# A decoder layer on one core: the cross-attention context as one product of 448 columns, its results in two bank halves, added on GpSimd

## The reference

```
q = rmsnorm((x @ Wq).reshape(b, s, H, D), gq)
k = rmsnorm((ctx @ Wk).reshape(b, Skv, H, D), gk)
v = (ctx @ Wv).reshape(b, Skv, H, D)
attn = softmax(einsum('bqhd,bkhd->bhqk', q, k) / sqrt(D))
out = einsum('bhqk,bkhd->bqhd', attn, v).reshape(b, s, H * D) @ Wo
```

## Time and profile before

| what | us |
|---|---|
| runs of the kernel | 1050.33 (median), 1049.07, 1054.15 |
| the profiled execution | 1048.38 |
| its span, first to last instruction | 1046.6 |
| PE, PEld busy | 1018.7, 909.6 |
| DVE, ACT, POOL busy | 725.7, 537.0, 531.0 |

### The profile page before, as it was taken

How to read it: one execution, slowest core, us unless ns; L and a number is a source line. 1 busy time by engine, 2 the same in 40 slices (tenths; PEclk the granted TensorE clock), 3 DMA queues, 4 the chain that set the end, 5 groups by cost and what they waited for, 6 DMA issues and landing times.

```text
span 1046.6 us, 20309 instructions
## 1 busy us (share of the span) xinstructions
PE 1018.7 (97%) x7021; PEld 909.6 (87%) x7021; DVE 725.7 (69%) x1496; ACT 537.0 (51%) x1075; POOL 531.0 (51%) x515
## 2 busy tenths in 40 slices
PE   8999989999999999999999999999999999999997
PEld 8866568899999999999999999999987888888885
DVE  4378866777767767776776776766886576666648
ACT  5355546655455455555554554555553346676610
POOL 1257857754644643634634634634474545544544
PEclk9999999999999999999999999999999999999999
DMA  8100104324323223233233233234220779999843
GB/s 299 62 32 2 61 18 157 150 109 155 115 107 114 100 107 117 96 111 115 94 116 109 99 118 104 103 116 132 103 90 1 278 284 380 388 400 388 303 116 115
DMA packets 45274, 153.46 MB, mean 147 GB/s; under 512 B 3769, under 2 KB 4793, under 8 KB 42145
## 3 DMA queue, kind: packets, MB, share of 16 engines
q1 hardware_dynamic: 42976, 145.38, 38.5%
q0 software_dynamic: 2240, 7.34, 2.1%
HBM read 130.04 MB, written 22.66 MB: 146 GB/s over the span
## 4 chain that ended last, share of the span: by engine, by line
PE 73%; POOL 4%; DVE 4%; issue 2%; ACT 1%; POOLq 0%; DVEq 0%; ACTq 0%
PE xa_y_ps L86 6%; PE xa_y_ps L88 5%; PE xa_y_ps L87 5%; PE ex_raw_gu_ps L86 5%; PE ex_raw_gu_ps L88 4%; PE ex_raw_gu_ps L87 4%; PE xa_c_ps L1965 4%; PE xa_c_ps L1961 4%; PE xa_c_ps L1960 3%; PE ex_raw_ey_ps L2187 3%; PE xa_turn_ps L2042 3%; PE xa_turn_ps L1998 3%; PE front_k_ps L86 3%; PE front_k_ps L88 3%; PE front_k_ps L87 3%
## 5 line engine op out<-in xcount | busy, mean ns | idle before, releaser
L1275 POOL TENSOR_TENSOR xa_probs<-xa_probs,xa_inv_sum 112x750 f32<-112x750 f32 x63 | 97.7, 1552 | 75.7 <-DVE xa_inv_sum L1615 75.7
L1564 DVE TENSOR_TENSOR xa_kT_lo<-xa_turn_ps,xa_kT_hi 128x750 fp32r<-128x750 f32 x63 | 59.2, 940 | 99.8 <-ACT xa_kT_hi L1363 99.7
L1260 POOL TENSOR_TENSOR k_ms<-k_ss,sum_eps 125x6 f32<-125x6 f32 x63 | 12.5, 198 | 210.9 <-DVE k_ss L1580 210.9
L1960 PE MATMUL xa_c_ps<-xa_probsT_hi,xa_nat 125*128 125x224 f32 x384 | 92.3, 274 | 2.7 <-ACT xa_probsT_hi L1379 2.7
L1961 PE MATMUL xa_c_ps<-xa_probsT_hi,xa_nat 125*128 125x224 f32 x384 | 92.3, 275 | 0.0
L1379 ACT CAST xa_probsT_hi<-xa_turn_ps 125x672 fp32r<-125x672 f32 x62 | 44.6, 720 | 87.3 <-PE xa_turn_ps L2042 87.3
L1263 POOL TENSOR_TENSOR k_inv<-k_ms,neg_half 125x6 f32<-125x6 f32 x63 | 83.4, 1324 | 8.3 <-POOL k_ms L1260 6.6
L1385 ACT ACTIVATE xa_probs<-xa_scores_ps,xa_bias,xa_q_scale 112x375 f32<-112x375 f32 x126 | 82.8, 663 | 5.9 <-DVE xa_bias L1590 4.7
L1960 PEld LDWEIGHTS xa_c_ps<-xa_probsT_hi,xa_nat 125*128 125x128 f32 x384 | 73.6, 192 | 3.5 <-issue 3.1
L1961 PEld LDWEIGHTS xa_c_ps<-xa_probsT_hi,xa_nat 125*128 125x128 f32 x384 | 73.5, 191 | 0.5
L86 PE MATMUL front_k_ps<-land_xa_wk_hi,land_xa_ctx 128*125 128x256 f32 x252 | 71.4, 283 | 1.5 <-DVE front_k_hat L1607 1.2
(11 more groups left out here) (406 smaller groups left out, 3545.8 us busy)
## 6 DMA issues: line engine op xcount, KB each, us to landing
xa_nat<-ctx_split SPq DMA_DIRECT2D x56, 750.0 KB
ex_raw_raw<-in_w_units SPq DMA_DIRECT2D x15, 1408.0 KB, 8.1
ex_raw_raw<-in_w_units SPq DMA_DIRECT2D x15, 768.0 KB, 8.0
land_ex_raw<-in_w_units SPq DMA_DIRECT2D x8, 1408.0 KB, 8.2
land_ex_raw<-in_w_units SPq DMA_DIRECT2D x8, 768.0 KB, 7.9
ctx_split<-xa_nat SPq DMA_DIRECT2D x8, 750.0 KB
sorted_x<-ex_raw_y_sb SPq DMA_DIRECT2D x7, 768.0 KB, 10.3
ex_raw_x_nat<-sorted_x SPq DMA_DIRECT2D x21, 256.0 KB, 8.4
```

The source lines that it names most:

```text
L1275: pool.tensor_tensor(probs[0:T, u % 2], probs[0:T, u % 2], inv_sum[0:T, u % 2, :].unsqueeze(2).broadcast_to([T, 2, KV]), ALU.mult).then_in ...
L1564: dve.tensor_tensor(kT_lo[:, :, 0:KV], turn_ps[:, :, 0:KV], kT_hi[:, :, 0:KV].bitcast(F32), ALU.subtract).then_inc(sem["kT_lo_done"], 1)
L1960: pe.matmul(c_view[:, c], nat[0:KT, u % 2, 0, at], probsT_hi[0:KT, :, cols], start=(t == 0), stop=False)
```

## The change

In units 8 to 61 the context product is done by `context_pairs`. The high and the low transposed probabilities of a unit now lie next to each other in one buffer, `probsT`. For each half `c`, the high context is multiplied with both in one matmul of 448 columns per third of the keys; the low context is multiplied with the high probabilities as before, in 224 columns. The result of a half `c` so has two parts of 224 columns: high x high plus low x high, and high x low. They fill a bank of their own: half 0 goes to `c_ps`, half 1 goes to the second bank of `turn_ps`.

In even units half 0 starts with the matmuls that need no low probabilities: three with the low context, one of the high context and the high probabilities; then come the wait for `probsT_lo_done`, one matmul of 224 columns and two of 448. Half 1, and both halves of odd units, are three of 448 and three of 224 columns, and begin behind the wait for `probsT_lo_done`.

ScalarE copies the first part of each half to `cT_hi` and the second part to a new buffer `c_second`. VectorE subtracts `cT_hi` from the first part of each half, into `c_rest`. GpSimd adds `c_rest` and `c_second` into `cT_lo`, first thing in its slot. TensorE waits at the turn of k for `c_rest_done` and `c_second_done` of the unit, since both read the second bank of `turn_ps` (`second_bank_read`). Units 0 to 7, 62 and 63 keep `context_of`.

```diff
-        probsT_hi, probsT_lo = sb("probsT_hi", [P, 2, KT_N * T], F32R), sb("probsT_lo", [P, 2, KT_N * T], F32R)
+        probsT = sb("probsT", [P, 2, 2, KT_N * T], F32R)
+        probsT_hi, probsT_lo = probsT[:, 0], probsT[:, 1]
+        c_second = sb("c_second", [P, CC, 2, T])
+        c_rest = y_sb[:, 1, 0:CC * 2 * T].rearrange("p (c h t) -> p c h t", c=CC, h=2)
...
+        c_pair = [bank[:, 0:4 * T].rearrange("p (l h t) -> p l h t", l=2, h=2) for bank in (c_ps, turn_ps[:, 1])]
...
             def slot(s, i):
+                u = s - 3
+                if B <= u < N:
+                    part = slice(u % 2 * T, (u % 2 + 1) * T)
+                    hold(pool, sem["c_rest_done"], i, CC * B, CC * (u - B + 1))
+                    hold(pool, sem["c_second_done"], i, CC * B, CC * (u - B + 1))
+                    pool.tensor_tensor(cT_lo[:, :, :, part], c_rest, c_second[:], ALU.add).then_inc(sem["cT_lo_done"], 1)
                 if s % B == 4 and s // B + 1 < PAIRS:
...
+                    for c in range(CC if u >= B else 0):
+                        hold(act, sem["c_ready" if c else "c0_ready"], i, B, u + 1)
+                        act.copy(cT_hi[:, c, :, u % 2 * T:(u % 2 + 1) * T], c_pair[c][:, 0]).then_inc(sem["cT_hi_done"], 1)
+                        hold(act, sem["cT_lo_done"], i, B, u)
+                        act.copy(c_second[:, c], c_pair[c][:, 1]).then_inc(sem["c_second_done"], 1)
...
-                    hold(dve, sem["cT_hi_done"], i, B, u + 1)
                     part = slice(u % 2 * T, (u % 2 + 1) * T)
-                    dve.tensor_tensor(cT_lo[:, :, :, part], c_view, cT_hi[:, :, :, part].bitcast(F32),
-                                      ALU.subtract).then_inc(sem["cT_lo_done"], 1)
+                    if u < B:
+                        context_low(u)
+                    for c in range(CC if u >= B else 0):
+                        hold(dve, sem["c_second_done"], i, CC * B, CC * (u - B) + c + 1)
+                        hold(dve, sem["cT_lo_done"], i, B, u)
+                        dve.tensor_tensor(c_rest[:, c], c_pair[c][:, 0], cT_hi[:, c, :, part].bitcast(F32),
+                                          ALU.subtract).then_inc(sem["c_rest_done"], 1)
...
+            context_halves(u - 2)
...
+            def context_sum(u):
+
+                part = slice(u % 2 * T, (u % 2 + 1) * T)
+                dve.wait_ge(sem["c_rest_done"], CC * (u - B + 1))
+                dve.wait_ge(sem["c_second_done"], CC * (u - B + 1))
+                dve.tensor_tensor(cT_lo[:, :, :, part], c_rest, c_second[:], ALU.add).then_inc(sem["cT_lo_done"], 1)
...
+            context_rest(u - 2)
...
+            context_sum(u - 2)
...
+            def context_pairs(u, i):
+
+                context_loaded(u, i)
+                if u == B:
+                    pe.wait_ge(sem["cT_lo_done"], B)
+                hold(pe, sem["c_rest_done"], i, CC * B, CC * (u - B) - 1)
+                hold(pe, sem["c_second_done"], i, CC * B, CC * (u - B) - 1)
+                hold(pe, sem["probsT_hi_done"], i, B, u + 1)
+                cols = [slice(t * T, (t + 1) * T) for t in range(KT_N)]
+                if u % 2 == 0:
+                    for t in range(KT_N):
+                        pe.matmul(c_pair[0][:, 0], nat_part(u, 1, 0, t), probsT_hi[0:KT, :, cols[t]], start=(t == 0), stop=False)
+                    pe.matmul(c_pair[0][:, 0], nat_part(u, 0, 0, 0), probsT_hi[0:KT, :, cols[0]], start=False, stop=False)
+                    hold(pe, sem["probsT_lo_done"], i, B, u + 1)
+                    pe.matmul(c_pair[0][:, 1], nat_part(u, 0, 0, 0), probsT_lo[0:KT, :, cols[0]], start=False, stop=False)
+                    for t in range(1, KT_N):
+                        mm = pe.matmul(c_pair[0], nat_part(u, 0, 0, t), probsT[0:KT, :, :, cols[t]], start=False, stop=(t == KT_N - 1))
+                    mm.then_inc(sem["c0_ready"], 1)
+                hold(pe, sem["probsT_lo_done"], i, B, u + 1)
+                for c in range(u % 2 == 0, CC):
+                    if c == 1:
+                        squares_taken(i, u + 2, 1)
+                    for t in range(KT_N):
+                        pe.matmul(c_pair[c], nat_part(u, 0, c, t), probsT[0:KT, :, :, cols[t]], start=(t == 0), stop=False)
+                    for t in range(KT_N):
+                        mm = pe.matmul(c_pair[c][:, 0], nat_part(u, 1, c, t), probsT_hi[0:KT, :, cols[t]], start=False,
+                                       stop=(t == KT_N - 1))
+                    mm.then_inc(sem["c_ready" if c else "c0_ready"], 1)
+
+            def second_bank_read(u, i):
+
+                hold(pe, sem["c_rest_done"], i, CC * B, CC * (u - B + 1))
+                hold(pe, sem["c_second_done"], i, CC * B, CC * (u - B + 1))
...
+                    if s - 3 >= B:
+                        second_bank_read(s - 3, i)
...
-                    context_of(u, i)
+                    if u < B:
+                        context_of(u, i)
+                    else:
+                        context_pairs(u, i)
...
+            second_bank_read(N - 3, 0)
```

47 lines of the change are left out of this document (32 added, 15 removed).

## The result

The changed kernel takes 1077.21 us (median of 1074.15, 1077.72, 1076.70 and 1078.47); the kernel before, with one more execution beside the three of the table, took 1051.68 us. The ratio is 1.0246 (95% interval 1.0220 to 1.0273): slower. The profiled execution took 1074.15 us against 1048.38, 25.8 us more, with a mean granted clock of 0.999 in both. The other three executions of the changed kernel were 2.6 to 4.3 us longer than the profiled one, and their mean granted clock was 0.997 or 0.998. So TensorE ran longer at its lower level in them; where, no trace shows.

The account below looks back on a forecast made before the run. TensorE's stream was taken as the bound (PE busy 97% of the span). Terms -6.4 + 4.6 + 4.7 + 21.3 (both stops) + 0.5 = 24.7 us, added to a median of 1050.33, gave 1075 us; range 1061 to 1090.

Parts of the forecast that it names:

- Merged matmuls: Context products, units 8 to 61: 297 mergers of two 224-column matmuls into one of 448 save 0.0214 us each, 6.4 us.
- The earlier wait for the low probabilities: Even units' context: the wait moves from behind six matmuls to behind four, costing 0.17 us each, 4.6 us in all.
- odd units ... pay nothing: Odd units' context: 12 query matmuls stand ahead of it, so the earlier wait costs nothing there.
- The second bank in an ordinary slot: Turn of k in ordinary slots: TensorE waits 0.1 us for the bank holding half 1, 4.7 us in all.
- a way to PE: From an end on DVE to PE's next weight load: at most 0.23 us, taken as 0.05.
- First stop: Split slots with wq: the sum delays POOL's queue, so TensorE waits 1.8 us for k_hat, in six slots.
- Second stop: Turn behind the split slot: TensorE waits 1.93 us for c_rest, queued behind wo_lo; net 1.5 us, seven times.
- the low end of the term: Turn behind the split slot: wo_lo at 1.42 us instead of 2.16 shortens the stop by 0.7 us, 5 us in all.
- Straight code: Code behind the loop: it takes its pieces twice more, for 0.5 us.
- the clock: Rival, split slots: two near stops lower TensorE's clock, 3 us more per split slot, 21 in all, 1096; chance 0.04.
- The other three: Rivals: bank waits in every slot (1089, chance 0.12); only the second stop (1064, 0.08); stops absent, faster side (1044, 0.10).

Follow-up runs that it names:

- e7: Changed kernel with each 448-column context product written as two of 224, same banks and waits: 1080.21 us, ratio 1.0283 to the kernel before.
- e10: e5 with the first context half of even units not merged, its six high-probability products ahead of the wait: 1046.06 us, ratio 0.9974 to the kernel before.
- e8: Kernel before plus only an unused 448-column GpSimd sum, behind a wait for the context's low part, heading six split slots: 1060.12 us, ratio 1.0105.
- e1: Changed kernel with GpSimd's split of wo's high part moved behind k_inv in every split slot: 1075.18 us, ratio 1.0234 to the kernel before.
- e3: Changed kernel with VectorE's split of wo's low part moved behind the context's subtractions in the next slot: 1071.52 us, ratio 1.0199 to the kernel before.
- e11: Changed kernel with only the last units (58 to 61) back in the form of before: 1067.65 us, ratio 1.0169 to the kernel before.
- e4: Changed kernel with both moves, wo's high part behind k_inv and its low part behind the context's subtractions: 1061.34 us, ratio 1.0109 to the kernel before.
- e9: Changed kernel with two unused VectorE reductions ahead of the first context subtraction in slot 37 and every eighth: 1082.29 us, ratio 1.0318 to the kernel before.
- e2: Changed kernel with VectorE's bias written as two instructions of one tensor input each: 1081.16 us, ratio 1.0282 to the kernel before.
- e5: Changed kernel with wo_hi on ScalarE, wo_lo behind c_rest, units 58 to 61 in the old form: 1047.93 us, ratio 0.9985 to the kernel before.

## Why the prediction came out as it did

The time was forecast at 1075 and measured at 1077.2, the profiled execution at 1073.1 and 1074.15. The mechanism is right; part of the closeness is luck, since errors cancel. By stage: up to slot 60 the terms gave some 22.5 us and 17.3 were measured (from one split slot to the next 3.7, and it was 3.0); for slots 61 to 64 they gave 2.2 and it was 5.8; for the experts nothing, and it was 3.1. The other half of the 2.2 us between forecast and median comes from the step from profile to median: 1.95 us was carried over from the kernel before, and in the changed kernel it is 3.06, in executions with a lower granted clock.

- **Merged matmuls, -6.4.** Right in kind and rate. The spacing is 0.203 us, and e7 gives 0.10 to 0.12 us a slot. The Trainium skill (TensorE: Matmul & The Clock Gate, "Back-to-back issue gap") has 2.5 ns a merger in a formula that it gives for an isolated matmul, and says that the formula under-counts short ones in a stream with weight loads; taken as the prediction took it, it would be 0.015 us a slot, and the runs show eight times that.
- **The earlier wait for the low probabilities, 0.17 us in even units.** Right: 0.17 in the rows, 0.19 by e7, and e10 got it back. The step that failed is "odd units ... pay nothing". It was read in slots with query products and carried to the last pair, which has none: there the wait grew by 1.24 and 0.99 us.
- **The second bank in an ordinary slot, 4.7.** Wrong in size: nothing. By e7 an odd slot pays 0.00. The fit put the end of `c_rest` 1.29 us into the slot, called it a draw against the turn's weight load at 1.33, and added a way to PE. In the changed kernel it ends 1.22 us into the slot (508.53 + 0.39 in slot 36) and the load stands at 1.35. This is most of the 5.2 us by which the term up to slot 60 was too dear.
- **First stop, 1.8.** Size 1.72 - 0.08 = 1.64 us, shown to be POOL's queue alone by e8, where it comes without the rest of the change, and by e1, where it goes. The lateness is the sum's wait and the sum together, 2.2 us. The place was wrong: 1.21 us stood inside the context product. The rows for seeing it were there: the bias has two SBUF inputs and came 0.67 us behind `wo_hi`, and POOL was to be 2.3 us late.
- **Second stop, 1.93 gross and 1.5 net.** PE's weight loads idle 1.80 us, its matmuls 1.59, and the slot pays 1.34 + 0.12 = 1.46. Cause shown by e3. `wo_lo` took 2.16 us as forecast; the 1.42 us that the low end of the term took for an undisturbed one, as twice a mean of half the width, was too long (1.08, see the last section).
- **Straight code, 0.5.** Too small: 1.31 at the first turn behind the loop, and 0.77 in slot 63, where the experts' split stands where `wo_lo` stands elsewhere. I had looked for the order of split and `c_rest` only in the pattern of eight slots. That the last pair cost some 8 us with its consequences is what e11 measured, with an uncertainty of 3.
- **The experts' stage, nothing foreseen.** In the profile PE waits there late for a weight split and a residual, where the kernel before has one such wait of 0.43 us:

```profile
1049.94 0.50 PE L86 MATMUL ex_raw_ey_ps<-land_ex_down_hi,ex_raw_h_hi 128*128 128x512 f32 x1 [0.98 <-DVE land_ex_down_lo L1690]
1055.89 0.50 PE L86 MATMUL ex_raw_ey_ps<-land_ex_down_hi,ex_raw_h_hi 128*128 128x512 f32 x1 [1.51 <-DVE resid L1785]
```

Ahead of them, until 1047.06, DVE stood idle for 3.9 us, waiting at the end for ACT, which had itself been idle for 6.3; for neither the profile names an engine. Behind slot 64 the profiles with the new form in the last pair are longer than the kernel before by 3.1 us (the change), 4.0, 4.2, 4.4 and 1.4 (e1 to e4), 0.6 (e9) and 0.2 (e7), those without it by 0.1 to 0.9. That the last pair drives this fits e11 but not e7 and e9; it stays open.

Of the rivals, the clock was nearest to more than a footnote. It didn't fall in the profiled execution of the changed kernel, and the lower means of the other three say that it did in them. With 0.5 to 0.6 us more of stop it fell in 8 of 13 slots (e1, e9), and then it cost mostly 1.5 us a slot, half of my estimate. The other three are excluded by the slot table.

## What to carry to other kernels

A step that is added at the head of a queue must be weighed in the one slot in which that queue has no gap, not in the mean: a wait and 1.15 us of GpSimd were free in seven slots of eight and cost 1.64 us of TensorE in the eighth. Before a pattern of slots is multiplied, look at its ends, where the work that covered a wait (here the next pair's queries) has run out. And when two stops stand close behind each other, cure the later one first or both: curing one alone can lengthen the other, and behind the longer stop the clock fell in half of the slots here (e1).

## What the runs showed of the hardware

**VectorE with two SBUF inputs waits for GpSimd.** The bias of two values took 1.55 us beside the split of `wo` and 0.16 alone; written with one tensor input it took 0.17 beside the same split (e2). `wo_lo` of 1024 columns took 2.16 us beside the scaling of the probabilities, 1.56 in e3 and 1.31 in e5, where less of it lay there. In e5 the scaling ends at 510.42 and `wo_lo` at 511.49:

```profile
508.98 1.44 POOL L1284 TENSOR_TENSOR xa_probs<-xa_probs,xa_inv_sum 112x750 f32<-112x750 f32 x1 [1.21 <-DVE xa_inv_sum L1656]
510.18 1.31 DVE L1031 TENSOR_TENSOR xa_wo_lo<-xa_wo_raw,xa_wo_hi 128x1024 fp32r<-128x1024 f32 x1
```

In each of these cases it ends 1.07 to 1.08 us behind the end of the scaling, from which I infer that 1.08 us is its own length; no run has it alone. The Trainium skill (SBUF — State Buffer, "Who interferes with whom") says that such an instruction and one of GpSimd that reads SBUF exclude each other, and that one SBUF input doesn't contend; these rows agree. The hold goes the other way too: GpSimd's `q_ms`, of four values, takes 0.20 us in slot 38 of the kernel before, but 1.18 in slot 37, where it ends just behind `wo_lo` (511.78 and 511.72):

```profile
510.60 1.18 POOL L1217 TENSOR_TENSOR xa_q_ms<-xa_q_ss,sum_eps 112x4 f32<-112x4 f32 x1
520.67 0.20 POOL L1217 TENSOR_TENSOR xa_q_ms<-xa_q_ss,sum_eps 112x4 f32<-112x4 f32 x1
```

Not every GpSimd instruction that reads SBUF held VectorE, however, and by the measurement the exclusion isn't general: `k_inv`, a power of six values, runs 1.33 us from 527.42 in slot 37 of the changed kernel, and the bias at 528.04 lies inside it with 0.16 us.

**The granted clock after a short stop.** Ahead of the turn, stops of 1.53 to 1.59 us left it at 1.00 seven times of seven; stops of 2.11 to 2.19 us brought it down to 0.50 for some 3 us in 8 of 13 cases, for 1.5 us each (about 1.0 in slot 61 of e9, where a later wait shrank from 2.46 to 1.87). Length alone doesn't decide: behind the wait of 2.46 us in slot 61 of the changed kernel it stayed at 1.00, behind one of 2.47 us in the same slot of e1 it fell; there, too, a wait of 2.26 us left it at 1.00 in e3 and brought it down in e4. In slot 63 of e11 it fell behind two waits of 0.90 and 0.47 us, which left it at 1.00 in the same slot of the kernel before.
